# The first group of attention by pairs of heads, with the second half's projections ahead of its row maxima

## What is computed

```python
# 1: self attention, 16 heads of 16 channels
q, k, v = split(layernorm(x) @ qkv_w.T + qkv_b)
scores = einsum('bhid,bhjd->bhij', q, k) / 4 - abs(i - j) * 0.5 ** head
x = x + (softmax(scores) @ v) @ out_w.T + out_b
# 2: cross attention over 77 context tokens, one head of 256 channels
x = x + (layernorm(x) + softmax(qc @ kc.T / 16) @ vc) @ Wo.T + bo
# 3: mixture of experts: 8 experts 256 -> 1024 -> 256, the best 2 of a token
x = x + sum_e weight[:, e] * (relu(layernorm(x) @ W1[e] + b1[e]) @ W2[e] + b2[e])
```

## Time and profile before

| | us |
|---|---|
| median of 3 runs (lowest, highest) | 1692.68 (1692.31, 1692.86) |
| the profiled execution, whole | 1696.51 |
| its span, first to last instruction | 1694.7 |
| TensorE busy | 1617.0 |
| VectorE busy | 1024.3 |
| ScalarE busy | 787.6 |
| GpSimd busy | 322.1 |

### The profile page before, as it was taken

The page is one execution under the profiler, slowest core; times in us unless marked ns, Lnnn a source line. Parts: engine busy times, 40 slices in busy tenths (PEclk is TensorE's granted clock), DMA queues, the critical chain, the costliest instruction groups (busy, mean ns, idle before and its releaser), DMA issues.

```text
span 1694.7 us, 29721 instructions
## 1 busy us (share of the span) xinstructions
PE 1617.0 (95%) x10022; PEld 968.4 (57%) x10022; DVE 1024.3 (60%) x2366; ACT 787.6 (46%) x1635; POOL 322.1 (19%) x310
## 2 busy tenths in 40 slices
PE   4889999999999999999999999989999999999997
PEld 2433343344454444444434453369998898999996
DVE  3688877888778778787788775333444232323332
ACT  2137666667646666655676657742221121212211
POOL 5301120001200041210031100332252121221221
PEclk9789999999999999999999999999999999999998
DMA  6930430333241440332431622335566665566662
GB/s 171 177 72 26 78 51 30 42 41 54 52 63 42 76 77 8 41 71 72 66 62 32 140 73 79 111 109 162 155 190 191 180 180 164 175 170 187 171 188 62
DMA packets 92661, 173.30 MB, mean 102 GB/s; under 512 B 13236, under 2 KB 51124, under 8 KB 92385
## 3 DMA queue, kind: packets, MB, share of 16 engines
q1 hardware_dynamic: 75376, 143.69, 33.9%
q0 software_dynamic: 15744, 26.54, 7.4%
q10 hardware_dynamic: 1392, 1.18, 0.3%
HBM read 133.69 MB, written 37.29 MB: 101 GB/s over the span
## 4 chain that ended last, share of the span: by engine, by line
PE 86%; DMA 5%; DVE 3%; ACT 3%; issue 2%; POOL 1%; SPq 0%; ACTq 0%; DVEq 0%; POOLq 0%
PE ps L1028 15%; PE ps L1054 14%; PE ps L1243 13%; PE ps L1014 13%; PE ps L1220 12%; DMA out<-yo,xi 3%; PE ps L1084 3%; DVE rmax L1392 2%; ACT prob L1255 2%; PE ps L1093 2%; PE ps L1106 2%; PE ps L1140 2%; PE ps L1075 2%; PE ps L1057 2%; PE ps L1017 2%
## 5 line engine op out<-in xcount | busy, mean ns | idle before, releaser
L1392 DVE TENSOR_REDUCE rmax<-ps 128x1 f32<-128x512 f32 x1024 | 664.7, 685 | 200.3 <-PE ps L1057 102.7
L1255 ACT ACTIVATE prob<-ps 128x512 f32<-128x512 f32 x1024 | 561.6, 600 | 336.3 <-PE ps L1017 184.3
L1054 PE MATMUL ps<-stacked_k,stacked_q 112*128 112x512 bf16 x1024 | 395.2, 390 | 15.7 <-DMA stacked_k<-parts_of_rows 7.4
L1014 PE MATMUL ps<-stacked_q,stacked_k 115*128 115x512 bf16 x1024 | 360.7, 383 | 7.3 <-ACT prob L1255 5.1
L1028 PE MATMUL ps<-prob,values 128*32 128x512 f32 x2048 | 274.0, 607 | 6.0 <-ACT prob L1255 5.5
L1243 PE MATMUL ps<-w,hidT 128*128 x1136 | 261.4, 384 | 8.1 <-issue 7.9
L1054 PEld LDWEIGHTS ps<-stacked_k,stacked_q 112*128 112x128 bf16 x1024 | 100.3, 98 | 292.3 <-DVE rmax L1392 207.6
L1220 PEld LDWEIGHTS ps<-xiT,w_now 128*128 128x128 f32 x2272 | 265.3, 192 | 3.5
L1220 PE MATMUL ps<-xiT,w_now 128*128 128x128 f32 x2272 | 267.1, 275 | 0.0
L1361 ACT ACTIVATE hidT<-ps,b 128x128 f32<-128x128 f32 x284 | 81.3, 369 | 356.2 <-PE ps L1220 356.2
L1243 PEld LDWEIGHTS ps<-w,hidT 128*128 128x128 f32 x1136 | 211.4, 191 | 40.7 <-issue 14.3
(11 more groups left out here) (181 smaller groups left out, 1134.3 us busy)
## 6 DMA issues: line engine op xcount, KB each, us to landing
w_now<-in_w SPq DMA_DIRECT2D x71, 1024.0 KB, 5.4
stacked_q<-parts_of_rows SPq DMA_DIRECT2D x90, 128.0 KB, 6.5
stacked_k<-parts_of_rows SPq DMA_DIRECT2D x90, 128.0 KB, 7.1
xi<-expert_rows SPq DMA_DIRECT2D x71, 130.0 KB, 2.1
w<-in_w SPq DMA_DIRECT2D x8, 1024.0 KB, 9.7
parts_of_rows<-q_part SPq DMA_DIRECT2D x21, 256.0 KB, 7.9
parts_of_rows<-k_part SPq DMA_DIRECT2D x21, 256.0 KB, 7.7
xr<-in_x POOLq DMA_DIRECT2D x4, 1024.0 KB, 9.7
```

The source lines that it names most:

```text
L1014: m = e.matmul(ps[:, bank, :], ka[i][0:ROWS, hh, kt * P:(kt + 1) * P], qa[i][0:ROWS, hh, ch * BANK:(ch + 1) * BANK], start=True, stop=True)
L1054: m = e.matmul(ps[:, bank, :], qa[i][0:MAX_ROW, hh, qt * P:(qt + 1) * P], ka[i][0:MAX_ROW, hh, kc * BANK:(kc + 1) * BANK], start=True, sto ...
L1255: e.activation(prob[:, u % NPROB, :], ps[:, u % NSCORE, :], ACT.Exp).then_inc(sem["exp"], 1)
L1392: e.tensor_reduce(rmax[:, G % 2, hh * NT + qt, kc:kc + 1], ps[:, p.bank("max", *k), :], AX.X, ALU.max).then_inc(sem["maxed"], 1)
```

## The change

It touches the opening and group 0; later groups are computed as before, and only the interleaving of their steps shifts a little.

- Group 0 goes by two pairs of heads. The maxima come as 16 for all four heads (first halves of queries and keys), then 24 for the first pair, then 24 for the second. `nmax`, `max_turn`, `nrow` and `max_rows` come once per pair, the first after 40 maxima.
- The scores of the first pair (32 units) come before those of the second. An attend takes two key tiles of two heads, and the four strips of the output are added pairwise by the turn: a matmul with a 128x64 matrix of two identities (`pair_sum`, in the unused tile `sc`) instead of a transpose. Group 0 has four `av`, `av_turn` and `on` instead of two.
- The second half's projections go ahead of the first maximum (`rows_in` holds the maxima back until the plan thinks that the rows have landed). ScalarE's reload of the second half of the keys is a step of its own (`first_reload`) between the evictions.
- `context_in` stands behind the second half's splits on GpSimd. The context's products start after the 40th maximum and go on beside group 0's scores. `late_in` stands behind the first `max_rows` on SP, and `route_setup` behind group 1's.
- In the main loop, `rows_given` makes maxima and side steps until the rows of the pair, or of group 1, have been put on the list. Next batch's steps may run in group 0, from 14 us after its first rows on, except while VectorE is late.

```diff
+    quadrant = lambda q, kc, heads: [(hh, NT // 2 * q + qt, kc) for hh in heads for qt in range(NT // 2)]
+    return quadrant(0, 0, range(HG)) + [one for pr in range(2) for q, kc in ((0, 1), (1, 0), (1, 1)) for one in quadrant(q, kc, pair_of(pr))]
+def pair_of(pr):
+    return range(2 * pr, 2 * pr + 2)
+FIRST_PAIR = UNITS // 4 + 3 * UNITS // 8
...
     def next_batches():
         for b in range(1, NB):
-            while now["ended"] < NG * (b - 1):
+            while now["ended"] < NG * (b - 1) or p.pe < landed + 14.0:
                 yield 0
...
     def row_maxima(G):
-        for hh, qt, kc in maxima_of(G):
+        for i, (hh, qt, kc) in enumerate(maxima_of(G)):
+            if (G, i) == (0, FIRST_PAIR):
+                add("nmax", 0, 0)
+                placing.append(row_place(0, 0))
...
-    add("context_in")
-    add("fetch_next", 1)
-    add("late_in")
...
+    rows_in = [p.emptied["low", 0, 0, 1, 0] + 8.0, p.emptied["low", 0, 0, 1, 1] + 11.0]
+    while beside or p.pe < landed:
+        if ("low", 0, 1, 1, 1) in p.number and ("context_in",) not in p.number:
+            add("context_in")
+            beside.append(context)
+        if ("high", 0, 1, 0, 1) in p.number and ("first_reload",) not in p.number:
+            add("first_reload")
+        while bank_free() and now["maxima"] < UNITS + LEAD and now["spread"] > now["maxima"] // UNITS and p.pe >= rows_in[now["maxima"] >= UNITS // 4]:
+            next(maxima)
         flush()
         if placing and not p.open:
             step_on(placing)
-            if not placing:
+            if not placing and landed > p.pe + 100.0:
                 landed = p.made["nrow"] + 4.0
-                add("route_setup")
+                add("fetch_next", 1)
+                add("late_in")
...
-    done = done_batches()
+    done = chain(context, done_batches())
...
+            if b == 0 and name == "next" and not p.open and p.at["dve"] > p.pe + 1.3:
+                continue
...
+    def rows_given(*key):
+        while ("max_rows", *key) not in p.number:
+            if bank_free():
+                next(maxima)
+            flush()
+            step_on(placing)
+            step_on(closing)
+            behind(0)
+            p.at["pe"] += 0.02
+    def order_of(G):
+        if G:
+            return [((ch, kt), [(ch, kt, hh) for hh in range(HG)]) for ch in range(NCH) for kt in range(NT)]
+        return [((NCH * pr + ch, two), [(ch, 2 * two + i, hh) for i in range(2) for hh in pair_of(pr)])
+                for pr in range(2) for ch in range(NCH) for two in range(NT // 2)]
     for G in range(NB * NG):
+        if G == 1:
+            rows_given(1, 0)
+            add("route_setup")
...
-                        m = e.transpose(ps[:, bank, q * P:(q + 1) * P], av[:, q * P:(q + 1) * P], ident[:, :])
+                        if G:
+                            m = e.transpose(ps[:, bank, q * P:(q + 1) * P], av[:, q * P:(q + 1) * P], ident[:, :])
+                        else:
+                            m = e.matmul(ps[:, bank, q * 2 * CT:(q + 1) * 2 * CT], av[:, q * P:(q + 1) * P], pair_sum, start=True, stop=True)
```

More of the change, by code:

```diff
@@ L10 @@
 from contextlib import ExitStack
+from itertools import chain
 import numpy as np
@@ L554, in plan @@
         next(opening)
-    add("context_in")
-    add("fetch_next", 1)
-    add("late_in")
     now["late"] = True
+    add("pair_sum")
     beside = [opening]
-    context = [context_products()]
-    maxima = row_maxima(0)
+    context = context_products()
+    maxima = all_maxima()
     landed = float("inf")
-    while beside or context or p.pe < landed:
-        if context and now["maxima"] >= UNITS // 2:
-            beside.append(context.pop())
-        while bank_free() and now["maxima"] < UNITS + LEAD and now["spread"] > now["maxima"] // UNITS:
-            if next(maxima, "end") == "end":
-                maxima = all_maxima()
+    rows_in = [p.emptied["low", 0, 0, 1, 0] + 8.0, p.emptied["low", 0, 0, 1, 1] + 11.0]
[7 more added lines that the diff above has]
+            next(maxima)
         flush()
@@ L574, in plan @@
             step_on(placing)
-            if not placing:
+            if not placing and landed > p.pe + 100.0:
                 landed = p.made["nrow"] + 4.0
-                add("route_setup")
+                add("fetch_next", 1)
+                add("late_in")
         elif beside and (p.open or p.room() <= p.pe + 0.3):
             side = beside.pop(0)
-            if next(side, "end") != "end":
+            if side is context and now["maxima"] < FIRST_PAIR:
+                beside.append(side)
+            elif next(side, "end") != "end":
                 beside.insert(0 if p.open else len(beside), side)
+        if beside == [context] and p.pe >= landed:
+            break
         p.at["pe"] += 0.02
+    while p.open:
+        next(beside[0])
     flush()
     now["running"] = True
-    done = done_batches()
+    done = chain(context, done_batches())
     coming = next_batches()
@@ L620, in unit @@
                 left = UNITS - now["maxima"] % UNITS
-                maximum(LEAD - min(left // 3, 8))
+                maximum(LEAD - min(left // 3, 8) if G else -2 * UNITS)
             flush()
@@ L627, in plan @@
         waiting = []
-        for ch in range(NCH):
-            for kt in range(NT):
-                for hh in range(HG):
-                    unit(ch, kt, hh)
-                    if hh == 2 and waiting:
-                        c_, k_ = waiting.pop(0)
-                        add("attend", G, c_, k_)
-                        if k_ == NT - 1:
-                            closing.append(finish(G, c_))
-                            step_on(closing)
-                    else:
-                        step_on(closing)
-                        behind(G // NG)
-                    maximum(0)
-                waiting.append((ch, kt))
+        for of, four in order_of(G):
+            if G == 0 and of[1] == 0:
+                rows_given(0, of[0] // NCH)
+            for n, one in enumerate(four):
+                unit(*one)
+                if n == 2 and waiting:
+                    c_, k_ = waiting.pop(0)
+                    add("attend", G, c_, k_)
+                    if k_ == (NT if G else NT // 2) - 1:
+                        closing.append(finish(G, c_))
+                        step_on(closing)
+                else:
+                    step_on(closing)
+                    behind(G // NG)
+                maximum(0 if G else -2 * UNITS)
+            waiting.append(of)
         add("attend", G, *waiting.pop(0))
         now["ended"] += 1
-        closing.append(finish(G, NCH - 1))
+        closing.append(finish(G, NCH - 1 if G else 2 * NCH - 1))
         step_on(closing)
```

132 lines of the change are left out of this document (75 added, 57 removed).

## The result

The changed kernel is slower, as forecast, and by more than forecast.

| chip | before, median us | changed, median us | ratio, 95% interval |
|---|---|---|---|
| first | 1692.49 (4 runs) | 1705.91 (1704.23 to 1707.51, 4 runs) | 1.0079 (1.0063 to 1.0094) |
| second | 1690.81 (21 runs) | 1702.31 (1696.75 to 1706.38, 6 runs) | 1.0058 (1.0038 to 1.0078) |
| third | 1692.65 (23 runs) | 1702.08 (1699.92 to 1709.54, 6 runs) | 1.0062 (1.0041 to 1.0082) |

A forecast was written before the change was run, and what follows sets the result against it. TensorE was taken as the bound, busy for 1617.0 of 1694.7 us. The terms -18.4 + 16.9 + 6.5 + 2.2 summed to +7.2 us, giving a forecast of 1699.9 us, slower, with a range of 1689.5 to 1704.

The forecast's parts named there:

- the wait that the text named: Ahead of the first score: rows queue behind group 2's spread, wait about 12 us, score at 92.4, 18.4 us earlier than before.
- The stall at the border: Ahead of score 65, between groups 0 and 1: TensorE waits 6.5 us for group 1's maxima rows, bounds 5 and 8.
- the half clock behind it: After the wait ahead of score 65: the clock at its lower level, 2.2 us lost.
- The value projection's wait of 5.3: In the opening: TensorE's 5.27 us wait for VectorE's split, behind GpSimd's issue of context loads, was to go.
- B: First score: the rows overtake the spread, score at 85.3, 7.1 us less, 1692.8 us, no change; chance 0.15.
- C: Border of groups 0 and 1: no stall, 6.5 + 2.2 us go, 1691.2 us, within no change; chance 0.13.
- D: First score: stores land before 63, score at 79.5, 12.9 us less, 1687.0 us, faster; chance 0.13.
- Part 2: TensorE work pushed behind the first score: 25 maxima 6.3, context 7.7, attended-value turns 2.8, maxima turn 0.1; sum 16.9 us.
- Part 3: Border of groups 0 and 1: stall of 6.5 us ahead of score 65, then 2.2 us lost to half clock.
- The other 16.5 us of that line: On SP ahead of the first score: 16.5 us from the first issue of group 2's spread to its last landing.
- Later: Behind score 65: 14 maxima fewer done, made up while TensorE is full; nothing added to the sum.
- Rival E: Group 0's scores: less other work beside them, ScalarE or VectorE paces TensorE, 3 to 6 us more, 1703 to 1706; chance 0.09.

The follow-up runs named there:

- e1: Changed kernel with the spread of group 2's maxima behind the first pair's maxima rows on SP; 1691.97 us, ratio 1.0011 to the kernel before.
- e3: Changed kernel with the opening's context steps and maxima going on for 14 us, not 4, after the pair's maxima are turned; 1691.31 us, ratio 1.0002.
- e2: Changed kernel with the wait ahead of score 65 filled with maxima and projections that otherwise stand behind it; 1696.94 us, ratio 1.003.
- e10: Changed kernel with maxima made to a lead in group 0, not only where a bank is free; 1697.25 us, ratio 1.0032.
- a_again: The changed kernel, unchanged, traced again on the second chip; 1702.31 us, ratio 1.0058 to the kernel before.
- b_again: The kernel before, unchanged, traced again; 1692.13 us, ratio 0.9999.
- e5: Changed kernel with the late loads put back ahead of the second half's stage stores on SP; 1703.41 us, ratio 1.008.
- a_third: The changed kernel, unchanged, traced on the third chip; 1702.08 us, ratio 1.0062 to the kernel before.
- b_third: The kernel before, unchanged, traced on the third chip; 1693.44 us, ratio 1.0004.
- e4: Changed kernel with the edits of e1 and e2 together; 1686.47 us, ratio 0.9971 to the kernel before.
- e8: Changed kernel without next batch's steps in group 0, which begin with group 1; 1704.08 us, ratio 1.0068.
- e6: Changed kernel with the edits of e3 and e2 together, both waits filled; 1685.5 us, ratio 0.9969 to the kernel before.
- e9: e6 without next batch's steps in group 0; 1691.8 us, ratio 1.0 to the kernel before.
- e11: Changed kernel with the edits of e10 and e1 together; 1686.09 us, ratio 0.9971 to the kernel before.
- e13: Changed kernel with the edits of e3 and e10 together; 1686.8 us, ratio 0.9973 to the kernel before.

## Why the prediction was right in direction and too small

**What held.** The first score has the wait that the text named, ahead of it the spread of group 2 on SP. It started at 89.9 where 92.4 was written, with a wait of 8.3 for "about 12"; the pair's maxima were complete at 72.07 (written: 72.5). The stall at the border was 7.06 (written: 6.5, bounds 5 and 8), with the cast at 1.17 again and the half clock behind it: the granted clock is at 0.50 from 172 to 182 us, the first matmuls take 0.61 in place of 0.38, and the shares of 0.60 and 0.89 make 4.0 and 1.1 us lost at the lower level's half rate, of which the part before 176.06 fell into the wait: about 3 us (written: 2.2). The value projection's wait of 5.3 is gone. e1, e3, e2 and e10 each remove one of the two waits, each by another edit, and gain 5.2 to 10.3 us at the last exponential (e10 against a_again of its chip, the others against the first trace; against the mean of the three traces e1, e3 and e2 gain 10.8, 12.2 and 7.2), so that these waits are shown as causes, and rivals B and C (no queue; no stall) have fallen. D, an early landing of the stores, has too: they landed at 73.5.

**Part 2.** From the first exponential to unit 128 the three traces of the kernel before take 126.8 to 127.2 us, the changed kernel's 154.7 to 155.1: 27.7 to 28.1 more by chip, where parts 2 and 3 gave 16.9 + 6.5 + 2.2 = 25.6. By lines, from the starts in b_again and in the changed kernel's first trace: the wait at the border 7.1; 18 maxima more, with their bands, 7.8; the context 8.7; the turns by pair 3.5 less 0.9; projections and transposes 1.9, some of it half clock behind the stall and 0.7 a wait for ScalarE. The 25 maxima of the forecast are 18 by then (49 in place of 74 at the first exponential, 207 in place of 214 at unit 128), but they cost 7.8 and not 4.5. Part 3 put 13.1 to 13.7 us between score 64 and the turn of group 1's maxima (its TensorE terms add up to about 12.3, not 13.7). The changed kernel's first trace takes 17.1 there, from 151.39 to 168.50 and at full clock, with waits for VectorE's reductions of 0.57, 0.51 and 0.51 and one of 0.7 for ScalarE that the sum did not have. The sum up to unit 128, +7.2, came out at 7.2 and, on the third chip, 6.8: the first score came 2.5 us earlier than written and what lies behind it took 2.1 to 2.5 longer, and that the two cancelled was luck. By the means of three traces it is 8.2.

**One term right for a wrong reason.** I had the spread of group 2 start 2 us earlier because the late loads no longer stood ahead of the stores. It started 4.0 earlier (73.46 for 77.49 in the earlier trace rows), but e5, with the loads ahead again, started it at 74.18. So the loads were not it. The other 16.5 us of that line, from the spread's first issue to the landing of what is issued behind it, came as written: 73.46 to 89.94. What holds the landing at 73.5 to 75.0, whenever the stores are issued between 53 and 67, stays open: by the stretches the DMA share was 1.05 from 50 to 70 us. That GpSimd's context loads now stand elsewhere was not tried alone.

**The step that failed** is the one headed "Later": 14 maxima fewer "are made up while TensorE is full", and nothing added behind unit 128. That is a term of the sum put at nothing, and it measured 4.2 to 5.8 us. Between units 128 and 512 the changed kernel takes 4.2 us (first chip) and 5.8 (second and third) more than 374.8. From unit 448 to 512 alone it is 60.6 in a_third for 56.9 in b_third. The stretches there, a_third and then b_third:

```profile
570.00:580.00 10.00, 10.00 (x78) 6.00 (x76) 7.46 (x14) 5.73 (x11) 0.00 (x0) 1.00 1.06 185
580.00:590.00 10.00, 10.00 (x48) 4.60 (x48) 6.21 (x21) 3.32 (x8) 0.00 (x0) 0.66 0.34 38
```
```profile
560.00:570.00 10.00, 10.00 (x78) 5.79 (x76) 7.65 (x13) 6.25 (x12) 0.00 (x0) 1.00 1.06 185
570.00:580.00 10.00, 10.00 (x69) 4.40 (x68) 8.03 (x23) 5.89 (x11) 0.00 (x0) 1.00 0.48 53
```

A share of 0.66 is 6.8 us at 1.2 GHz, half of which, 3.4 of the 3.7 us, is lost. The first trace has 58.9 there, with the clock low for half as long:

```profile
580.00:590.00 10.00, 9.96 (x57) 3.43 (x56) 7.07 (x22) 5.14 (x10) 0.00 (x0) 0.83 0.30 34
```

The clock falls in this place in the three traces of the changed kernel and in e1, e2, e4, e5 and e8 (58.9 to 60.6 us from unit 448 to 512), and in none of the three of the kernel before, nor in e3, e6, e9, e10, e11 and e13 (56.7 to 57.4). So, as far as 17 traces tell, whether it falls goes with the order of the steps; no wait shows it, and how long it stays low differs between executions of one order: 1.7 or 3.4 us lost. The other 2.1 us of the 5.8 lie between units 192 and 256 (1.5) and 320 and 384 (1.2), with 0.6 less elsewhere. They are three more maxima and bands (3 x 0.28 = 0.8), and 1.3 us that I can't name. e10, e11 and e13 lose 5.0 to 6.9 us between units 128 and 512 without the fall; e10 has projections of next batch there that the kernel before makes earlier (3.8 us by the starts). None of these runs takes the fall of the clock out alone, so its price is read from the traces and not from an experiment.

**The sum again**, in the pair from one chip: first score 20.9 earlier (111.3 less 90.4), 27.7 more by unit 128, 5.8 more by unit 512, nothing behind it: +12.6 at the last exponential, and +12.2 in the spans. The ratio of the timed runs there, 1.0062, is 10.5 us. On the first chip the traces differ by 9.4 us and the medians by 13.4: the traced execution of the kernel before lay 3.8 us above its median, that of the changed kernel (1706.0) at its own, and I had carried the 3.8 over. Rival E named a time of 1703 to 1706, where the result lies, but by waits for ScalarE and VectorE; TensorE's waits for VectorE's reductions in the first trace are 5.4 us in all, fewer than the 7.0 before, though 1.6 of them lie in the border's stretch; behind unit 128 it was the clock, more maxima and what stays unnamed. The chance for "slower", 0.57, was if anything low.

## What to carry to other kernels

An early start of a stage is worth only the idle time that it removes. Two orders that started their scores 12.7 us apart ended alike; two that differed in an 8 us wait differed by 9 to 10. So look first at what TensorE has to do while the rows of a reduction travel, and whether small transfers stand in a queue behind large ones; put the small ones first, or fill the wait. A moved block must also be followed to the end of the stage in which it is made up, with the granted clock of each stretch. By order alone, with its two waits filled, the changed kernel is 0.3% faster than the kernel before (e6: 0.9969, 0.9954 to 0.9983), as are e4, e11 and e13.

## What the runs showed of the hardware that I had not expected

**The clock fell with no idle moment in the profile.** TensorE was busy for 10.00 of 10 us in both stretches of a_third above, and yet the clock went to the lower level, within the second of two sets of 16 router matmuls of eight columns (timeline of PE):

```profile
577.00 1.90 PE L1216 MATMUL ps<-wr,xT 128*128 128x8 f32 x16
578.76 0.38 PE L1118 MATMUL ps<-stacked_k,stacked_q 112*128 112x512 bf16 x1
...
579.53 3.02 PE L1216 MATMUL ps<-wr,xT 128*128 128x8 f32 x16
582.40 0.59 PE L1118 MATMUL ps<-stacked_k,stacked_q 112*128 112x512 bf16 x1
```

The set takes 3.02 in place of 1.90, and maxima 0.59 in place of 0.38 behind it. b_third has the same two sets, 0.68 us from the end of the one to the start of the next (0.63 here), at the full clock throughout. The Trainium skill (TensorE: Matmul & The Clock Gate, Part 1: The HAM clock gate) says that the clock is low by default and that activity releases it. Here it fell while the profile shows TensorE active throughout, so that rule gives no reason for this fall by what the profile counts; what in the order decides whether it falls, no run here shows.

**A cast of 32x128 took 0.21 or 1.17 us.** At the border it started at 170.85 and ended at 172.02; GpSimd's operation on split parts ran from 170.79 to 171.94. In the opening, with GpSimd idle, it is 0.21. The Trainium skill (SBUF — State Buffer, Terms) describes a port pair shared by VectorE and GpSimd, held for a whole instruction while the other is blocked; the two ends, 0.08 us apart, agree.

**Identical instructions scatter.** From the last exponential on every kernel here has the same 3750 matmul instructions, and the rest took 574.7 to 584.6 us in 17 traces.
